# Expert attention: the keys padded by head are written by ScalarE, straight from PSUM

## The reference, cut to what matters

```python
sx = jnp.einsum('bsh,ndh->bnsd', x, hl_w) + hl_b[None, :, None, :]
q = jnp.einsum('bnsd,neod->bneso', sx, wq)
k = jnp.einsum('bnsd,nod->bnso', sx, wk)
v = jnp.einsum('bnsd,nod->bnso', sx, wv)
scores = jnp.einsum('bnesd,bntd->bnest', q, k) * d ** 0.5 + causal
att = jax.nn.softmax(scores, axis=-1)
qkv = jnp.einsum('bnest,bntd->bnesd', att, v)
```

## Time and profile before

| | |
|---|---|
| median of three timed runs | 2035.8 us |
| the profiled execution | 2043.5 us, its span 2041.7 us |
| TensorE busy | 1719.6 us (84%) |
| VectorE busy | 1488.7 us (73%) |
| ScalarE busy | 755.0 us (37%) |
| GpSimd busy | 690.7 us (34%) |

### The profile page before, as it was taken

The page is one execution under the profiler, slowest core; times in us unless marked ns, Lnnn a source line. Parts: engine busy times, 40 slices in busy tenths (PEclk is TensorE's granted clock), DMA queues, the critical chain, the costliest instruction groups (busy, mean ns, idle before and its releaser), DMA issues. The chain is left out here.

```text
span 2041.7 us, 45613 instructions
## 1 busy us (share of the span) xinstructions
PE 1719.6 (84%) x15064; PEld 1344.5 (66%) x15064; DVE 1488.7 (73%) x4423; ACT 755.0 (37%) x2274; POOL 690.7 (34%) x957
## 2 busy tenths in 40 slices
PE   1499999999689999999999999946999997888990
PEld 1266666666567777777777777735888887777780
DVE  6276766666537888898898988876666664988881
ACT  2254445454234443434343444312222222433440
POOL 2522222222144544555545445432121112222210
PEclk9999999999789999999999999955555555988885
DMA  2000000000000000000000000000000000000001
GB/s 112 1 2 0 0 0 0 0 0 0 1 1 1 2 1 0 0 0 0 0 0 0 0 0 0 1 0 1 0 0 0 0 1 1 1 0 0 0 2 30
DMA packets 6952, 8.13 MB, mean 4 GB/s; under 512 B 6244, under 2 KB 6244, under 8 KB 6756
## 3 DMA queue, kind: packets, MB, share of 16 engines
q1 hardware_dynamic: 6884, 7.25, 1.0%
HBM read 5.71 MB, written 1.54 MB: 4 GB/s over the span
## 5 line engine op out<-in xcount | busy, mean ns | idle before, releaser
L1143 ACT ACTIVATE ex_pT<-ex_T 128x376 f32<-128x376 f32 (+1 forms) x384 | 162.4, 439 | 217.4 <-PE ex_T L1045 208.1
L605 ACT ACTIVATE al_prob<-al_S,al_negmax 94x94 f32<-94x94 f32 (+1 forms) x512 | 146.0, 375 | 180.2 <-DVE al_negmax L732 180.2
L1208 DVE TENSOR_REDUCE ex_negmax<-ex_R 94x2 bf16<-94x376 f32 (+1 forms) x384 | 186.8, 543 | 30.5 <-PE ex_R L1016 30.0
L1045 PE MATMUL ex_T<-ex_qm,ex_kpad 128*128 128x188 f32 x1024 | 189.8, 329 | 0.0
L506 PE MATMUL al_S<-al_kpad,al_qT 128*94 128x376 f32 x384 | 166.5, 516 | 0.0
L1045 PEld LDWEIGHTS ex_T<-ex_qm,ex_kpad 128*128 128x128 f32 x1024 | 163.1, 192 | 5.1
L945 POOL TENSOR_SCALAR_AFFINE_SELECT ex_pT<-ex_pT 128x512 f32<-128x512 f32 x128 | 84.4, 660 | 236.6 <-ACT ex_pT L1143 236.6
L683 POOL TENSOR_TENSOR al_kpad<-al_kT,al_quad_mask 128x1504 f32<-128x1504 f32 x32 | 86.2, 2693 | 186.1 <-ACTq L620 186.1
L732 DVE TENSOR_REDUCE al_negmax<-al_S 94x2 f32<-94x376 f32 (+1 forms) x192 | 99.1, 542 | 62.5 <-PE al_S L507 56.6
L1555 POOL TENSOR_TENSOR ta_kk<-ta_ext 94x320 f32<-94x320 f32 x64 | 60.4, 962 | 246.4 <-DVE ta_qkn L1735 163.0
L1028 PE MATMUL ex_R<-ex_sxT,wsb 128*128 128x188 f32 x256 | 72.2, 364 | 47.5 <-DVE ex_negmax L1208 47.5
(11 more groups left out here) (308 smaller groups left out, 4301.0 us busy)
## 6 DMA issues: line engine op xcount, KB each, us to landing
tok_xin<-x_t SPq DMA_DIRECT2D x4, 760.0 KB, 6.5
wsb<-weights SPq DMA_DIRECT2D x1, 2531.0 KB, 13.9
out<-stream SPq DMA_DIRECT2D x2, 752.0 KB
tok_par<-tok_w SPq DMA_DIRECT2D x1, 4.5 KB, 1.6
```

The lines of the kernel that those rows point to most:

```text
L605: last = nc.scalar.activation(p[:, k, cols], S[0:P, k, cols], ACT.Exp, bias=negmax[g % 2][:, m:m + 1])
L1045: last = nc.tensor.matmul(T[:, k, (j % 2) * N:(j % 2 + 1) * N], kpad[par][:, j, 0:K0], qm[e % 2][:], start=True, stop=True)
L1143: nc.scalar.activation(pT[e % 2][rows, k, cols], T[rows, k, cols], ACT.Exp)\
L1208: red(dst, src, AX.X, ALU.max, negate=True).then_inc(sem["r_used"], 1)
```

## The change

`kT` and its semaphore are gone, and so are GpSimd's two products of each row. In place of ScalarE's one copy stand eight passes, four into `kpadb` and then four into `kpad`, each for one head: the scale is a per-partition column of `key_scale` (4 in that head's quad, 0 elsewhere), the bias a column of `key_one` (1 in that head's extra row). Both tables are made once, by two small GpSimd instructions. X counts as read when the last of the eight passes is done (`USES` names `kpad_ready`, which counts two for each row). ScalarE waits before the passes, on `t_full`, until the scores of the row that last used the same buffers were computed.

```diff
--- before.py
+++ after.py
@@ -796,6 +796,8 @@
         quad_mask = sb("quad_mask", [128, NH])
         one_row = sb("one_row", [128, 1])
+        key_scale = sb("key_scale", [128, NH])
+        key_one = sb("key_one", [128, NH])
...
-        kT = sb("kT", [128, N])
...
@@ -873,8 +874,8 @@
-        USES = {"k": "kT_ready"}
-        PER_ROW = {"sx": 2, "v": 2}
+        USES = {"k": "kpad_ready"}
+        PER_ROW = {"sx": 2, "v": 2, "k": 2}
@@ -915,6 +916,8 @@
+            const(nc.gpsimd.tensor_scalar(key_scale[:], quad_mask[:], D ** 0.5, None, ALU.mult))
+            const(nc.gpsimd.tensor_scalar(key_one[:], quad_mask[:], one_row[:], None, ALU.mult))
@@ -949,13 +952,6 @@
-                    r = t - FRONT
-                    if e == 1 and valid(r):
-                        pool.wait_ge(sem["kT_ready"], r + 1)
-                        for dst in (kpadb, kpad):
-                            nc.gpsimd.tensor_tensor(dst[1 - u][:], kT[:].unsqueeze(1).broadcast_to([128, NH, N]),
-                                                    quad_mask[:].unsqueeze(2).broadcast_to([128, NH, N]), ALU.mult)\
-                                .then_inc(sem["kpad_ready"], 1)
@@ -1147,8 +1143,12 @@
                     if e == 1 and valid(rf):
                         act.wait_ge(sem["k_full"], rf + 1)
-                        need(act, sem["kpad_ready"], 2 * rf)
-                        used("kT_ready", kT[:], ALL, slice(0, N), ACT.Identity, bias=one_row[:], scale=D ** 0.5)
+                        need(act, sem["t_full"], 3 * NE * (rf - 1))
+                        for dst in (kpadb[odd], kpad[odd]):
+                            for n in range(NH):
+                                ins = nc.scalar.activation(dst[:, n, :], X[:, 0:N], ACT.Identity,
+                                                           bias=key_one[:, n:n + 1], scale=key_scale[:, n:n + 1])
+                            ins.then_inc(sem["kpad_ready"], 1)
```

More of the change, by code:

```diff
@@ L845, in expert_attention @@
         X = psum("X", [128, 512])
-        names = """consts stats_set settled aggregate stats_ready var_set rstd_ready xn_ready kT_ready kpad_ready
+        names = """consts stats_set settled aggregate stats_ready var_set rstd_ready xn_ready kpad_ready
             xT_full xT_used sx_full sx_used k_full q01_full q01_used q23_full q23_used v_full v_used m_full m_used
@@ L852, in expert_attention @@
         sem = {n: ctx.enter_context(nc.semaphore("ex_" + n)) for n in names}
-        CONSTS = 21
+        CONSTS = 23
         DEPTH = 7
```

## The result

The changed kernel takes 2177.86 us (median of four runs, 2173.05 to 2181.24) against 2037.32 for the kernel before, timed beside it: a ratio of 1.0682, interval 1.0651 to 1.0714. That is 140.5 us slower. The forecast was 127 us (2163), and its range of 2108 to 2205 holds the measured time.

What follows compares the result with a forecast made beforehand. TensorE and VectorE were taken to hand work to each other in a ring. A stall of 82 us plus 45 us of clock falls made 127 us, on the 2035.8 median 2163 us, range 2108 to 2205.

Steps and rivals of the forecast that it cites:

- Who waits: TensorE's fc1 waits for kpad_ready, and its in-order work waits behind; net 2.74 us a turn, 82 us in all.
- the wait of 0.45 us: TensorE's wait for the maxima of e=3, before that query product, disappears: 0.45 us gained per turn.
- The price of the block: Eight ScalarE passes at a 0.44 us step take 3.61 us in place of kT's 0.42, 3.19 us later.
- the bound of 0.32: Lower bound on the ScalarE pass step, from the one-pointer kT copy out of PSUM: 0.32 us.
- The clock: TensorE's pause before fc1 drops its clock once per turn: 1.5 us (1.23 to 2.5) in 30 turns, 45 us.
- The stall without the clock: Rival: TensorE stalls before fc1 but its clock stays up; 2118 us, chance 0.10.
- A: Rival: TensorE stalls but its clock stays up, 2118 us, chance 0.10.
- Cheap passes: Rival: ScalarE passes step at 0.32 us; 2127 us with clock falls, 2090 without; chance 0.13.
- VectorE as the bound: Rival: VectorE's freed L1272 time, 98 us over 32 turns, comes out as speed; 1938 or 2021 us, chance 0.04.
- rival C: VectorE is the bound; its freed 3.05 us per turn, 98 us over 32 turns, becomes speed; chance 0.04.
- the list of what is queued behind the block on ScalarE: After the passes on ScalarE comes the qm copy of e=2, at 1110.6, claimed not late for scores(2).

Runs made afterwards that it cites:

- filled pause: Changed kernel plus 34 TensorE matmuls into unused columns of bank O, between queries(2) and fc1, results unused: 2116.37 us, ratio 1.0385 to the kernel before.
- the second experiment: Against the changed kernel: X copied once into kT, all eight passes made from kT directly after, ahead of the queries copy: 2136.21 us, 1.0476 to the kernel before.
- sixteen passes: Changed kernel with eight more ScalarE passes in the block, into spare tensors that nothing reads: 2293.17 us, ratio 1.1246 to the kernel before.

## Why the prediction was right

*Who waits.* Right as put: fc1 behind `kpad_ready`, TensorE's order behind fc1, no slack between fc1 and the query product of e=3, the wait of 0.45 us gone, the other two left. Holding X with no other edit gives 2187.59 us, giving it back early gives 2024.7.

*The price of the block.* 3.61 us forecast, 3.29 measured: a step of 0.40 us, not 0.44, between the bound of 0.32 and the row that I chose. A pass out of PSUM with two pointers takes 528 ns, as tok_above did, so the duration was right and the overlap was too small. Net of the 0.45 us: 3.29-0.42-0.45 = 2.42 us forecast by the measured block, 2.45 by the turns with a filled pause, 2.74 in the sum.

*The clock.* The mechanism was right and the size was too small. Forecast 1.5 us a turn; the turns of the changed kernel last 28.62 and those with the pause filled 26.54, so it is 2.08 us. What was off is the number of stretches at half speed, not the price of one. Of the 25 turns sixteen have one stretch at half speed and last 28.03 us on average, 1.5 more than with the pause filled, as forecast; nine have two and last 29.66, 3.1 more. I had one fall a turn in the sum and named the second as the upper end; here are 34 stretches in 25 turns. (In six of the nine turns the clock stays down for 6.8 us in one piece, in three it falls twice.) The two errors, -0.29 and +0.58, leave 0.29 us a turn, and the trace shows 4.50 against the 4.24 of the forecast. That the sum comes so near is in part luck: a stall put too high hides part of a clock term put too low. The last key block starts 127.5 us later than the last kT copy did; the two profiled spans differ by 129.6 us, the medians of the timed runs by 140.5, and each kernel's runs spread by 8 us. The remaining 11 us lie within that spread: the profiled execution before was the slowest of its four (2043.52), the one after the fastest of its four (2173.05). I have no row that says what makes one execution slower than another.

*The rivals.* The stall without the clock (2118) is what the filled pause made: 2116.37. In the changed kernel itself the clock did fall, so A is out. Cheap passes: half true, 0.40 in place of 0.44. VectorE as the bound: VectorE gave up 72 us of busy time and TensorE gained 0.43 us a turn from it where X was free. The 98 us of rival C took the median for every turn; the 34 instructions had held VectorE for 88.2 us in all, 2594 ns on average. The Trainium skill, SBUF — State Buffer, Who interferes with whom, says that VectorE and GpSimd block one another over a shared port pair; the trace agrees (408 ns at the median without GpSimd's products, 3220 with them). VectorE was really held up, but at a time when TensorE had work of its own.

*What I left out.* In the list of what is queued behind the block on ScalarE stood the copy of the queries, not the copy of fc1. In the changed kernel it makes no difference, since fc1 itself is late. It decided the second experiment.

## What to carry to other kernels

A PSUM bank through which many products pass is a queue: what an operation costs there is the time for which it holds the bank, not its engine's busy time. One copy out of the bank and all further work from SBUF beat both kernels, 2024.5 us, with the passes placed where no copy out of the bank waits behind them. Before moving work to an idle engine, list everything that stands behind the new place in that engine's order, and who waits for each of it. And a pause on TensorE is to be priced twice: the pause itself, and the work after it at half clock. In the changed kernel that second part is 2.08 us a turn on 2.45 us of stall; it isn't a rate, for the 3.18 us of pause that sixteen passes add bring only 0.5 us more of it.

## What the hardware showed that I had not expected

ScalarE passes of the same size and the same 528 ns, with two pointers each, follow one another at 0.44 us in tok_above, which reads SBUF, and at 0.40 in kpad, which reads PSUM; a duration alone doesn't give the step. The two differ in their function too (Relu and Identity), so it isn't shown that the place they read from is the reason. With one scale pointer from SBUF four passes take 1.46 us, a step of 0.34. The skipped fall after a pause of 1.88 us comes in every fourth turn (811.93, 917.84, 1023.73 and so on to 1341.33), with the same instructions in each, so a pause of a given length doesn't decide by itself whether the clock falls; I can't say from these runs what does. The trace before had it already: of twelve pauses of 1.20 us at full clock in the attention layer ahead of this one (166 to 481 us, L490), five were followed by a fall within 2 us and seven by none for over 29 us. And filling a pause with matmuls that nobody reads gave back 61.5 us: in 25 turns one stretch at half speed was left of the 34.
